# A software pipeline of eight groups: where the router's counts, scatters and last weights stand

## The reference, cut to what matters

```python
x = x + _L0_attn_ref(_layernorm(x), Wq, Wk, Wv, Wo, bo)        # linear attention, 16 heads, causal
x = x + _L0_xattn_ref(_layernorm(x), ctx_1024, mask, wq, wk, wv, wo)   # 77 context tokens, 16 heads
x = x + _L0_ffn_ref(_layernorm(x), gate_w, w1, w2)             # 16 experts, two for each token
```

```python
probs = jax.nn.sigmoid(logits)
top_vals, sel = jax.lax.top_k(probs, K)                        # K = 2
weights = top_vals / (top_vals.sum(-1, keepdims=True) + 1e-06)
ranks = (running count of earlier tokens that chose the same expert)
slot = jnp.where(ranks < capacity, flat_sel * capacity + ranks, sentinel)   # capacity = 640
padded = zeros.at[slot].set(x_rep)                             # rows go to their expert's slots
h = gelu(padded @ w1); out_padded = h @ w2                     # for each expert
out = (out_padded[slot] * weights).sum(over the two choices)
```

## Time and profile before

| what | value |
|---|---|
| three runs | 1647.87, 1657.05, 1658.19 us |
| the profiled execution | 1666.73 us |
| its span | 1664.7 us |
| PE busy | 1514.0 us (91%) |
| DVE busy | 1014.5 us (61%) |
| ACT busy | 900.2 us (54%) |
| POOL busy | 473.1 us (28%) |
| mean granted clock of PE | 0.958 |

### The profile page before, as it was taken

How to read it: one execution, slowest core, us unless ns; L and a number is a source line. 1 busy time by engine, 2 the same in 40 slices (tenths; PEclk the granted TensorE clock), 3 DMA queues, 4 the chain that set the end, 5 groups by cost and what they waited for, 6 DMA issues and landing times. The chain is left out here.

```text
span 1664.7 us, 26844 instructions
## 1 busy us (share of the span) xinstructions
PE 1514.0 (91%) x9735; PEld 1071.9 (64%) x9735; DVE 1014.5 (61%) x2312; ACT 900.2 (54%) x2289; POOL 473.1 (28%) x625
## 2 busy tenths in 40 slices
PE   8999999898977889999999899999999989996299
PEld 5766777676656767787777566666666654442288
DVE  3657878888886335222222566766664568777883
ACT  4457786675786222211212555666656633597980
POOL 3212334344345300000002665555533300032100
PEclk9999999999997899999999999999999979998599
DMA  4441111111241144333424211110100000000031
GB/s 120 153 160 25 39 38 40 37 51 51 82 133 45 58 154 136 123 114 125 152 90 137 71 39 52 41 35 28 39 14 14 1 26 1 0 0 18 21 101 64
DMA packets 105281, 109.33 MB, mean 66 GB/s; under 512 B 29762, under 2 KB 94156, under 8 KB 105152
## 3 DMA queue, kind: packets, MB, share of 16 engines
q1 hardware_dynamic: 99008, 91.06, 17.8%
q0 software_dynamic: 6144, 16.57, 3.1%
HBM read 65.81 MB, written 42.01 MB: 65 GB/s over the span
## 5 line engine op out<-in xcount | busy, mean ns | idle before, releaser
L2121 ACT ACTIVATE c_pr<-bank,c_nmax 128x256 f32<-128x256 f32 x256 | 117.7, 472 | 118.0 <-DVE c_nmax L2238 117.9
L1827 POOL TENSOR_SCALAR c_pr<-c_pr,c_rsum 128x256 f32<-128x256 f32 x256 | 127.6, 514 | 186.4 <-DVE c_rsum L2243 186.0
L1558 ACT ACTIVATE b_G<-bank 128x320 f32<-128x320 f32 x128 | 55.9, 437 | 210.4 <-PE bank L1507 210.4
L1507 PE MATMUL bank<-b_XT,shared 128*128 128x320 f32 x512 | 154.2, 436 | 0.0
L2238 DVE TENSOR_REDUCE c_nmax<-bank 128x2 f32<-128x512 f32 x128 | 82.4, 686 | 105.8 <-PE bank L1886 102.5
L1521 PE MATMUL bank<-shared,b_G 128*128 128x256 f32 x640 | 142.2, 379 | 0.0
L959 ACT ACTIVATE a_L<-a_L,a_Lm 128x77 f32<-128x77 f32 x512 | 131.2, 353 | 4.4 <-DVE a_Lm L1097 4.3
L1521 PEld LDWEIGHTS bank<-shared,b_G 128*128 128x128 f32 x640 | 120.9, 190 | 17.8
L508 POOL TENSOR_TENSOR a_Pm<-a_L,a_xrden 128x1024 f32<-128x1024 f32 x32 | 61.3, 1916 | 220.6 <-DVE a_xrden L1104 220.6
L1507 PEld LDWEIGHTS bank<-b_XT,shared 128*128 128x128 f32 x512 | 92.2, 192 | 27.4 <-issue 1.0
L1577 DVE COPY b_Y<-bank 128x256 f32<-128x256 f32 x80 | 34.0, 425 | 119.8 <-PE bank L1521 119.6
(11 more groups left out here) (386 smaller groups left out, 3433.1 us busy)
## 6 DMA issues: line engine op xcount, KB each, us to landing
shared<-L_ffn_w SPq DMA_DIRECT2D x32, 512.0 KB, 6.1
t_slots_in<-a_h SPq DMA_DIRECT2D x20, 512.0 KB, 6.2
shared<-t_slots_in SPq DMA_DIRECT2D x15, 640.0 KB, 7.0
t_slots_out<-b_Y SPq DMA_DIRECT2D x15, 640.0 KB, 4.1
hT_all<-x SPq DMA_DIRECT2D x8, 512.0 KB, 3.8
a_xr<-x SPq DMA_DIRECT2D x8, 512.0 KB, 3.9
t_x_a<-a_x SPq DMA_DIRECT2D x8, 512.0 KB, 2.9
shared<-t_x_a SPq DMA_DIRECT2D x8, 512.0 KB
```

Source lines behind the costliest of these rows:

```text
L1507: t = p.matmul(P[2 + n % 2][:, 0:HC], w1[e % 3][:, u, 128 * f:128 * f + 128], XT[e % 2][:, u, HC * m:HC * m + HC], start=(u == 0), stop=(u ...
L1827: p.tensor_scalar(pr[k][:, e, u, :], pr[k][:, e, u, :], rsum[k][:, e, u:u + 1], 1.0, ALU.mult, ALU.mult).then_inc(q.pr_ready, 1)
L2121: a.activation(pr[t % 2][:, e, u, :], P[e][:, S * u:S * u + S], ACT.Exp, bias=nmax[t % 2][:, e, u:u + 1], accum_out=sums[t % 2][:, e, u:u ...
```

## The change

Four things move; nothing is added or taken away.

1. POOL: the two `scatter` calls go from slots 0 and 1 to slots 1 and 2. Since the first now stands behind slot 1's `normalised`, the 8 transfers of a group follow each other. The pipeline gets one step more at its end for it.
2. PE: `ranks` goes from slot 6, ahead of `states`, to slot 7, behind `x_turn`. In `UNITS` its bank goes to the same place, behind the three units of `x_turn`.
3. DVE: `count_ranks` goes from slot 6 to the end of slot 7, behind `shifts(2)`, just ahead of `place_tokens`.
4. DVE: for the last group `weigh` is done right behind `place_tokens`, ahead of the additions of the last later units (line 1309; 1310 after the change).

```diff
-        FIRST, LAST = -2 * NS + 2, (NG + 4) * NS + 2
+        FIRST, LAST = -2 * NS + 2, (NG + 4) * NS + 3
...
                  6: (("proj0", 0), ("turn1a", -1), ("turn1b", -1), ("turn0a", 2), ("turn0b", 2),
-                     ("rank", -4), ("state0", 1), ("state1", 1)),
-                 7: (("val3", 0),) + tuple((n, -2) for n in turned(1)) + (("xq0", -1), ("xvm", -1), ("xvl", -1))}
+                     ("state0", 1), ("state1", 1)),
+                 7: (("val3", 0),) + tuple((n, -2) for n in turned(1)) + (("rank", -4), ("xq0", -1), ("xvm", -1), ("xvl", -1))}
...
-                    if s in (0, 1) and there(g - 5):
-                        scatter(g - 5, s)
+                    if s in (1, 2) and there(g - 5):
+                        scatter(g - 5, s - 1)
...
-                        if back4:
-                            ranks(g - 4)
...
                     if s == 7:
                         if back2:
                             x_turn(g - 2, 1)
+                        if back4:
+                            ranks(g - 4)
...
-                    if s == 1 and there(g - 5):
+                    if s == 1 and there(g - 5) and g - 5 < NG - 1:
                         weigh(g - 5)
...
-                        if back4:
-                            count_ranks(g - 4)
...
                         if back4:
+                            count_ranks(g - 4)
                             place_tokens(g - 4)
+                            if g - 4 == NG - 1:
+                                weigh(g - 4)
```

## The result

| | before | changed |
|---|---|---|
| median, first session | 1657.62 us (6 runs, 1647.87 to 1659.18) | 1665.68 us (6 runs, 1664.94 to 1672.35) |
| ratio, 95% interval | | 1.0080 (1.0061 to 1.0098) |
| profiled execution, span | 1666.73, 1664.7 us | 1664.94, 1663.0 us |

The change made the kernel slower by 0.8%. The two medians stand only 8.1 us apart, but the ratio of 1.008 is 13.3 us. A second session with 29 runs of before gave 1.0083, with medians 13.7 us apart, so I reckon with 13 us. The forecast was 1662 us, +5.

A forecast was written before the change was run, and what follows sets the result against it. PE bounds the kernel from 625 us; in the drain DVE's order, with the engines it waits for, sets the pace. 1.3 + 7.1 - 3.5 = +4.9, say +5 us, gave 1662 us, range 1649 to 1674.

The forecast's parts named there:

- the slow clock spreads: Rival: PE's clock in 475 to 500 us falls from 0.98 to 0.70; +11, 1668 us; chance 0.2.
- row of eight, periods 5 to 7: Period 5, before the drain: one_of_two and `deviation(0)` pushed back behind the longer row of scatters, +0.4 us.
- row of eight in the drain, and the bank: Scatters and bank wait move period 10's PE transpose by +7.1 us; bank waits in periods 5 and 6 cost 0.9.
- last weights: End of the layer: with `weigh` out of SP's way, the experts start earlier, -3.5 us (-3.5 to -2).
- The failed step: Period 5: one_of_two and `deviation(0)` pushed back behind the longer row of scatters, priced at 0.4 us.
- Part 1: `ranks` behind `x_turn`: M waits vanish in periods 8 and 9, freed PE time worth nothing; slot 7's `masked` -1.3 us.
- Part 2 and 3, the drain's chain: Eight scatters delay period 8's slot 3 product 3.1 us; slot 0 awaits `rank`'s bank; period 10's transpose moves +7.1.
- near the slow end: Period 9's `x_scores` after the bank wait: 497.4 at full clock, 500.4 all at the slow rate, taken as 499.7.
- Part 4: End of the layer: SP's loads go when the scatters land, PE is last, experts at 592.6 us, -3.5 us.
- The scatter has 3.9 us to land: End of the layer: last scatter issued by 585.2 us, SP's loads take 2.3, so SP should not end last.
- the rival of chance 0.08: End of the layer: scatters land so late that SP still ends last; -3.5 shrinks to about 0, +8.5, 1665.5 us.
- The row of scatters: Rival, slot 3 of periods 8 and 9: eight transfers finish before the reciprocal; -3.3, 1654 us; chance 0.2.

The follow-up runs named there:

- the scatters alone: Kernel before with only the scatters moved to slots 1 and 2, eight in a row behind slot 1's product: 1661.83 us, ratio 1.0054.
- the row in periods 5 to 7: Kernel before with the eight scatters in a row behind slot 1's product in periods 5 to 7 only: 1659.76 us, ratio 1.0026.
- the last weights alone: Kernel before with only the last group's `weigh` moved right behind its `place_tokens`: 1651.09 us, ratio 0.9988.
- the row in the drain: Kernel before with the eight scatters in a row behind slot 1's product from period 8 on only: 1657.30 us, ratio 1.0021.
- sums first: Kernel before with only the rank counts moved, DVE summing them first in slot 7, ahead of the shifts: 1651.26 us, ratio 0.9994.
- the counts alone: Kernel before with only `ranks` and `count_ranks` moved as in the change, DVE summing last in slot 7: 1656.35 us, ratio 1.0040.

## Why the prediction was right, and which term was not

Within 1%, the sign and the range (1649 to 1674) held. The size did not: +4.9 forecast, +13 measured. That 1665.68 lay in the range is owed to the range's width, which was set for a rival (the slow clock spreads) that did not come.

| term | predicted | measured by a run of its own |
|---|---|---|
| row of eight, periods 5 to 7 | +0.4 | +4.3 (2.5 to 6.1) |
| row of eight in the drain, and the bank | +7.1, and +0.9 before the drain | +3.5 (0.8 to 6.1) and +6.6 (4.0 to 9.1) |
| last weights | -3.5 | -2.0 (-4.3 to +0.5) |
| sum | +4.9 | +12.4 |

**The failed step** is the sentence "With one_of_two and `deviation(0)` pushed back behind the longer row of scatters in period 5, I add 0.4". I had seen that the row pushes them back and priced it by feel. The row adds four transfers of 1.28 us ahead of both. In the run with the scatters alone `deviation(0)` then ended at 306.59, DVE stood idle for 1.02 us and lost 1.74 more beside POOL's product, and PE waited 2.2 us longer and restarted slow. This could have been worked out as in period 8, but for the 1.74: no row of before has a shift that starts beside a product. Period 5 is not all of it. From slot 1's product to that of the next period, period 5 takes 65.42 and 67.31 us in the two runs that have the row there (the scatters alone, and the row in periods 5 to 7), and 61.61 and 61.45 in two that don't (the last weights alone, the row in the drain); period 7 takes 51.87 and 51.89 against 49.55 and 49.59. So some 2.3 us stand in period 7, for which the prediction had nothing; no run isolates them. Over the three periods the four traces differ by 6 to 9 us, more than the 4.3 by time.

**Part 1 was right.** The waits for M in periods 8 and 9 went, and the run with sums first, which frees PE just as much, won 1.0 us (-3.3 to +1.5). PE's wait went to Pl. The 1.3 us that DVE no longer does ahead of `masked` are in the traces: from slot 1's product of period 8 to slot 7's products of periods 8 and 9 it is 28.64 and 66.16 us with the last weights alone, and 27.32 and 63.49 with the sums first, 1.3 us less for each period. The prediction gives them back at the end of the slot; with the sums first they are kept. So the order of the sum is worth more than the bank's net loss: 6.2 us of the drain, of which some 3.7 are loss and 2.6 a gain forgone.

**Part 2 and 3, the drain's chain, came out within 0.3 us at each step.** Measured from the product of slot 1 in period 8 (459.32 before, 462.98 changed):

| step | predicted | in the traces |
|---|---|---|
| slot 3's product, period 8 | +3.1 | 12.60 - 9.44 = +3.2 |
| `masked`, slot 7 | +1.8 | 25.90 - 23.83 = +2.1 |
| `x_scores`, period 9 | +8.3 | 40.06 - 32.08 = +8.0 |
| slot 3's product, period 9 | +11 | 58.45 - 47.68 = +10.8 |
| slot 1's product, period 10 | +7.1 | 83.26 - 76.01 = +7.3 |

The bank was awaited for 4.92 us ("some 5 us"). Behind it only the four matmuls of line 622 ran at the slow rate (3.56 against 1.88 us); lines 723 and 727 took 1.03 and 1.07 us, as before. From `xq1` to `x_scores` it took 5.35 us, where the prediction had 6.0 (493.7 to 499.7), "near the slow end"; the bank came 0.3 us later than forecast, and the two errors cancel in part. (The prediction's bounds for this step, 5.8 and 9.5, are 6.1 and 9.1 by its own figures.) The granted clock was 0.79 in 487 to 495 us of the run with the counts alone, behind its wait, and 1.00 in 481 to 489 us with the sums first, behind its own. The Trainium skill ("TensorE: Matmul & The Clock Gate", The HAM clock gate) has idle PE fall to half its clock; the trace agrees with 3.54 against 1.98 us for the same four matmuls.

The same distance to period 10's product in the runs with one part each: 80.02 us with the counts alone (456.32 to 536.34), 80.15 with the row in the drain alone (453.83 to 533.98), and 76.37 with neither (457.01 to 533.38, the last weights alone). So the bank gives 3.7 and the row 3.8 of the 7.3. With the row in all periods and the old counts it is 78.45, so there the row's share is only 2.1. Where the rest of the counts' 6.6 us stands is less sure: from period 5's slot 1 product to 456.32 that run takes 170.00 us, against 168.21 and 166.89 in two runs whose steady part is that of before, but with the sums first it is 169.32 and 167.48. PE's waits for L1198 before 455 us are 2.4 us in that run and none with the sums first; the prediction had 0.9 for them.

**Part 4 did some two thirds of what it says in the traces** (by time -2.0 is not clear of zero). "The scatter has 3.9 us to land" failed. In the profiled execution the last scatter left the queue 6.2 us ahead of PE's end (585.19 and 591.35), behind the stall at 569.45. In the traces without the stall it is 1.7 to 2.5 us (580.27 and 582.29 with the row in the drain alone, 579.72 and 582.20 with the last weights alone). SP's loads need 1.38 + 2.22 us behind it, so they end last: in part the rival of chance 0.08. Won were 2.35 us of the 3.5.

**The rivals.** The row of scatters was not hidden: the two products behind the rows (475.58 and 521.43) had no idle time ahead of them. The slow clock did not spread beyond what was counted (0.81 in place of 0.98 in 475 to 500 us, but 0.84 in place of 0.70 in the next window, so 0.83 against 0.84 over both). The price that the rival gave, +11, lay near the truth for another reason.

## What to carry to other kernels

A row of short operations that is moved behind a product delays everything behind it on its queue, in every period and not only in the one with the longest wait: work out each follower's new time, and who reads it. When a unit takes a rotating bank, look for the reader that frees it and put that reader first in its slot: one sum's place was worth 6 to 8 us in the drain's traces here. Cutting such a row in pieces, each where the queue stood idle, turned +8.9 into -3.8 us.

## What the runs showed of the hardware

- **A short DVE instruction took as long as POOL's product beside it.** The shift L1146, with two inputs in SBUF, has a median of 0.16 us over 24 instances in the changed kernel, and took 1.88 us where it began 0.04 us after POOL's product (302.62 for 1.91). DVE ended 0.01 us behind it. All five traces with the row in period 5 show this (1.88 or 1.89 us); in the nine traces without it no shift between 200 and 400 us is over 0.17. The Trainium skill ("SBUF — State Buffer", SBUF: two separate sides) says that the two engines share a pair of ports, which goes to whichever starts first for its whole instruction, and that a DVE instruction with two SBUF inputs needs it against a GpSimd one that reads SBUF; the trace agrees with the ends 0.01 us apart. No run isolated it.
- **Loads behind scatters started 1.37 or 1.38 us after the last scatter left POOL's queue** in all seven traces with the last weights at once (592.98 - 591.61 in the changed kernel, 581.10 - 579.72 with the last weights alone).
- **One profiled execution had stalls of its own**, on DVE, ACT and PE at the same moments, named "remote" or "issue" in the trace. At the three places DVE was idle for 2.87, 3.07 and 8.92 us, against 1.09, 0.54 and 5.32 in the run with the last weights alone: some 8 us more, by my estimate. None of the 13 other traces has a wait named "remote" in the first 600 us on these engines. Their cause is open; the lesson is to compare distances within a trace.
